# Attention's unit 0 on one core: two of the four key copies are issued by GpSimd instead of SyncE

## The chip, the core and the metric

The kernel runs on one NeuronCore of one Trainium2 chip. A core has five engines that run side by side and meet at semaphores: TensorE (PE, matmuls; PEld is its weight load), VectorE (DVE), ScalarE (ACT), GpSimd (POOL) and SyncE (SP), which here only issues DMAs. The metric is the device time of one execution in microseconds.

## The reference, cut to what matters

The program is two blocks on an `x` of 8 x 512 x 256: an mLSTM-like mixing layer and an MLP, then a cross-attention of 16 heads of 64 and a mixture of 8 experts. The change lies in the cross-attention, which reads a context of the same shape:

```
q = query @ W_Query + B_Query ; k = key @ W_Key + B_Key ; v = value @ W_Value + B_Value
scores = jnp.einsum('bqhd,bkhd->bhqk', q, k) / D ** 0.5
probs = jax.nn.softmax(scores, axis=-1)
out = jnp.einsum('bhqk,bkhd->bqhd', probs, v)
return out.reshape(B, Lq, H * D) @ W_Output + B_Output
```

## The kernel before, in words

Attention (`attention`, L835 to L1290) works through 64 units: 8 batches times 8 pairs of heads. One unit u makes queries, keys and values of two heads (`project`, `project_values` on PE), then 8 score tiles of 128 queries x 512 keys, four per head. Each tile goes PE (`score`, L978), DVE row maximum (L1199), ACT exponential (L1133), DVE reciprocal (L1204), GpSimd scaling (L1174), PE transpose (L991), and a copy to SBUF (L1211 on DVE, L1152 on ACT). Then come values (`weigh_values`) and the output map. The loop is software-pipelined: unit u+1's projections and unit u-1's tail are laid between unit u's score tiles, in an order written out by hand for each engine.

Scores are computed from numbers split in two parts, high and low, so that a matmul over 128 rows holds 64 rows of the one and 64 of the other. The keys come out of PE for both heads at once, 64 partitions each. ACT writes the high part into `k_own[:, 0]` (L1093) and counts `kh`; DVE writes the low part into `k_own[:, 1]` (L1193) and counts `kl`. Then four DMAs (L929, 64 partitions x 4 KB = 256 KB each) copy them into `k2`: head 0, partitions 0 to 63 of `k_own`, to partitions 0 to 63 and to 64 to 127 of `k2`; then head 1, partitions 64 to 127, to both halves likewise. SyncE issues all four, in that order, for each unit, and the first score of a unit waits for all four (L975). `k_own` has one buffer: ACT waits for a unit's copies before it writes the next unit's keys (L1092).

Unit 0 is apart, since nothing is ahead of it to cover its start. PE projects keys, queries and values of unit 0 (L1046 to L1048) and turns the last batch's input (`turn_in`, L1042), then stands at the first score. At that time DVE normalises the last batch (statistics L1251 to L1258, then four instructions at L1263), which needs GpSimd's power (L1167), and makes the low part of the queries (L1186, counts `ql`, for which the first score also waits). GpSimd, after its power, waits for L1263 and adds a bias to the last batch (L1170), then begins the scaling of the tiles (L1174). SyncE, after unit 0's four copies, issues the loads that the attention needs later: the rest of the three projection weights (L907, 768 KB each), the output weights (L909, 1 MB) and the gate weights (L912, 4 bytes at a time).

Of the kernel before, what the change touches and what calls it, by code (L numbers as in the profile page):

```python
# [11 lines left out]
F32 = mybir.dt.float32  # L12
# [4 lines left out]
ALU = mybir.AluOpType  # L17
# [4 lines left out]
P = 128  # L22
B, S, D = 8, 512, 256
N = B * S
TPB = S // P
# [5 lines left out]
AH, AD = 16, 64  # L31
HP = AH // 2
# [13 lines left out]
def sems(ctx, nc, phase, names):  # L46
    return {n: ctx.enter_context(nc.semaphore(f"{phase}_{n}")) for n in names.split()}


def wait_apart(eng, sem, value):  # L50

    eng.wait_ge(sem, value)
    eng.nop(nofuse=True)  # L53
# [313 lines left out]
def wait_count(eng, sem, value):  # L367

    if value > 0:
        eng.wait_ge(sem, value)  # L370
# [462 lines left out]
def attention(nc, c, x_all, xnT_all, ctxT_all, first, after_s, Wq, Wk, Wv, Wo, gate_w, lg, rows, rows_in, out, landed):  # L833
# [3 lines left out]
    with ExitStack() as ctx:  # L837
# [6 lines left out]
        k_own = sb("k_own", [P, 2, S], F32R)  # L844
        k2 = sb("k2", [P, 2, 2, 2, S], F32R)
# [13 lines left out]
        S_BANK, T_BANK, A_BANK, O_BANK, Y_BANK = 0, 2, 4, 6, 7  # L859
        s = sems(ctx, nc, "at", "w scaled q_ps qh ql k_ps kh kl k2 v_ps V s_ps nmax exp rinv pn t_ps "  # L860
                 "pt_v pt_a pv oT y_ps x gT stats mv ve rstd xn tx_ps xT l_ps lg "
                 "in_stats in_mv in_ve in_rstd in_xn in_added in_tx_ps in_xT")
        w_dram = [W.rearrange("(c p) n -> p c n", p=P) for W in (Wq, Wk, Wv)]
        wo_dram = Wo.rearrange("(a p) d -> p a d", p=P)
        ON_ACT = (4, 5)
# [11 lines left out]
        def routed(u, r):  # L877

            return u // HP - 1 if u >= HP and u % HP == r else None

        NORM, APPLY, TURN, GATE, LAST = 1, 2, 3, 4, B - 1
# [20 lines left out]
        with nc.Block() as block:  # L902
            @block.sync
            def _(sp):
                def load_weights():
                    for k in range(3):
                        sp.dma_start(w_rest[:, k, :, :], w_dram[k][:, :, W_EARLY * P:HP * P]).then_inc(s["w"], 16)  # L907
                    sp.wait_ge(first["loaded"], 16 * 6)
                    sp.dma_start(wo_s[:, :, :], wo_dram).then_inc(first["loaded"], 16)  # L909
                    with nc.allow_non_contiguous_dma("8 gate weights per row"):  # L910
                        for k in range(DC):
                            sp.dma_start(gT[:, k, :], gate_w.rearrange("e (k p) -> p k e", p=P)[:, k, :]  # L912
                                         ).then_inc(s["gT"], 16)

                def store_rows(b):
                    sp.wait_ge(s["xn"], b + 1)
                    rv = rows.rearrange("(b k h p) d -> b p k h d", k=2, h=2, p=P)
                    for k in range(2):
                        sp.dma_start(rv[b, :, k, :, 0:D], ctxT_all[:, k, b * S:b * S + S].rearrange(
                            "p (h d) -> p h d", d=D)).then_inc(rows_in, 16)  # L920
                    sp.dma_start(out[0:N, :].rearrange("(b t p) d -> b p t d", p=P, t=TPB)[b],
                                 x_all[:, b * TPB:(b + 1) * TPB, :]).then_inc(landed, 16)

                for u in range(U):
                    sp.wait_ge(s["kh"], u + 1)
                    sp.wait_ge(s["kl"], u + 1)
                    for h in range(2):
                        for half in range(2):
                            sp.dma_start(k2[AD * half:AD * half + AD, u % 2, h, :, :].bitcast(F32),  # L929
                                         k_own[AD * h:AD * h + AD, :, :].bitcast(F32)).then_inc(s["k2"], 16)  # L930
                    if u == 0:
                        load_weights()
                    if routed(u, TURN) is not None:
                        store_rows(routed(u, TURN))
                store_rows(LAST)

            @block.tensor
            def _(pe):
# [32 lines left out]
                def score(u, j):  # L971
                    wait_count(pe, s["exp"], NBL * u + j - 1)
                    if j == 0:
                        pe.wait_ge(s["ql"], u + 1)
                        pe.wait_ge(s["k2"], 64 * (u + 1))  # L975
                    h, q = j // TPB, P * (j % TPB)
                    for part in range(2):
                        ins = pe.matmul(ps[:, S_BANK + j % 2, :], q2[:, u % 2, h, q:q + P], k2[:, u % 2, h, part, :],  # L978
                                        start=part == 0, stop=part == 1)
                    ins.then_inc(s["s_ps"], 1)  # L980
# [69 lines left out]
                for u in range(U + 1):  # L1050
                    for j in range(NBL):
                        if there(u):
                            score(u, j)
                            if j >= 2:
                                turn(u, j - 2)
                        if j < 2 and there(u - 1):
                            turn(u - 1, NBL - 2 + j)
                        if j < 2 and there(u + 1):
                            project(u + 1, j)
                        if j == 2 and there(u - 1):  # L1060
                            weigh_values(u - 1)
                        if j == 4 and there(u + 1):
                            project_values(u + 1)
                        if j in (5, 6) and there(u - 1):
                            output(u - 1, j - 5)
                        if j in (3, 7) and there(u):
                            if j == 3 and there(u + 1) and u % HP in (TURN, GATE):
                                pe.wait_ge(s["kl"], u + 2)
                            if routed(u, TURN) is not None:
                                turn_rows(routed(u, TURN), j // 4)  # L1070
                            if routed(u, GATE) is not None:
                                if routed(u, GATE) == 0 and j == 3:
                                    pe.wait_ge(s["gT"], 16 * DC)
                                map_gates(routed(u, GATE), j // 4)
# [6 lines left out]
            def _(act):  # L1081
# [7 lines left out]

                def keys(u):  # L1090
                    act.wait_ge(s["k_ps"], u + 1)
                    wait_count(act, s["k2"], 64 * u)  # L1092
                    act.activation(k_own[:, 0, :], ps[:, A_BANK + 1, :], ACT.Identity,  # L1093
                                   bias=b_s[:, 1, u % HP:u % HP + 1]).then_inc(s["kh"], 1)

# [24 lines left out]

                act.wait_ge(s["scaled"], 1)
                keys(0)
                queries(0)
                values(0)
# [34 lines left out]
            @block.gpsimd  # L1159
            def _(pool):  # L1160
                def spread(b):
                    wait_apart(pool, s["ve"], b + 1)
                    pool.tensor_tensor(rstd[:, :], ve[:, :], c["minus_half"][:, 0:TPB], ALU.pow
                                       ).then_inc(s["rstd"], 1)

                wait_apart(pool, s["in_ve"], 1)
                pool.tensor_tensor(rstd[:, :], ve[:, :], c["minus_half"][:, 0:TPB], ALU.pow).then_inc(s["in_rstd"], 1)  # L1167
                wait_apart(pool, s["in_xn"], 1)
                x_last = x_all[:, LAST * TPB:(LAST + 1) * TPB, :]
                pool.tensor_tensor(x_last, x_last, after_s[:, :].rearrange("p (a d) -> p a d", a=1).broadcast_to(  # L1170
                    [P, TPB, D]), ALU.add).then_inc(s["in_added"], 1)
                for n in range(NBL * U):
                    wait_apart(pool, s["rinv"], n + 1)
                    pool.tensor_scalar(Pr[:, n % 4, :], Pr[:, n % 4, :], rinv[:, n % 4:n % 4 + 1], 1.0,  # L1174
                                       ALU.mult, ALU.mult).then_inc(s["pn"], 1)
                    if n % NBL == NBL - 1 and routed(n // NBL, NORM) is not None:
                        spread(routed(n // NBL, NORM))
                spread(LAST)

            @block.vector  # L1180
            def _(dve):
# [31 lines left out]

                def add_out(u, half):
                    dve.wait_ge(s["y_ps"], 2 * u + half + 1)
                    if u == LAST * HP:
                        dve.wait_ge(s["in_added"], 1)
                    at = (u // HP) * TPB + 2 * half
                    xv = x_all[:, at:at + 2, :].rearrange("p t d -> p (t d)")
                    dve.tensor_tensor(xv, ps[:, Y_BANK - half, :], xv, ALU.add).then_inc(s["x"], 1)  # L1220
# [583 lines left out]
```

## Time and profile before

| | us |
|---|---|
| median of 3 runs (lowest, highest) | 1828.46 (1826.79, 1832.12) |
| the profiled execution's own time | 1826.98 |
| its span | 1825.2 |
| PE busy | 1657.8 (91%) |
| DVE, ACT, POOL busy | 1209.9, 842.8, 606.4 |
| the key copies (L929), 256 issues, issue to landing | 4.1 |

The span is what the trace covers; the execution takes 1.8 us more. Attention lies from about 427 us to 1597 us in it. Idle time is told with what ended it: `<-DMA at_k<-at_k_own` means that the copy from `k_own` to `k2` was the last thing that the engine waited for. A DMA has two times: that of the instruction which issues it, and that from its issue to its landing, when the semaphore has its full count. PEclk is the clock that the throttle granted to TensorE, 1.00 for 2.4 GHz and 0.50 for 1.2 GHz.

### The profile page before, as it was taken

The page shows a single profiled execution, that of the slowest core. Times are in us where ns is not written, and L with a number is a line of the kernel's source. Part 1 is how long each engine was busy: PE and PEld are TensorE (multiplying, and loading weights), DVE is VectorE, ACT ScalarE, POOL GpSimd, SP SyncE. Part 2 cuts the span into 40 slices and gives each one's busy share as a digit, 9 for nine tenths or more (in the row PEclk, how much of TensorE's full clock was granted, in tenths as well). Part 3 has the DMA queues.
Part 4 walks back from the last instruction along what each step waited for, and adds up shares of the span by engine and source line. Part 5 has one row for each costly group of instructions (what it writes and reads, how often), then busy time and mean ns, then how long its engine had stood idle before and what let it go on. Part 6 is the DMA issues. An engine that isn't in the chain of part 4 may idle for free. (4 is left out here: it accounts for less than half of the span.)

```text
span 1825.2 us, 25796 instructions
## 1 busy us (share of the span) xinstructions
PE 1657.8 (91%) x8789; PEld 1126.1 (62%) x8789; DVE 1209.9 (66%) x2690; ACT 842.8 (46%) x1870; POOL 606.4 (33%) x730
## 2 busy tenths in 40 slices
PE   6569999998999999999999999999999999973583
PEld 4447777756666666666666666666666666642352
DVE  6445655534777777777777786777777777748770
ACT  3324343433555555555555555555555555531110
POOL 2144444431232323322332332232332333220485
PEclk9669999999999999999999999999999999985697
DMA  8100000004222323232322232232323232213244
GB/s 261 31 24 12 12 12 1 1 0 122 51 66 53 87 47 70 47 93 47 70 70 62 54 88 53 52 88 47 70 47 93 47 70 70 57 37 98 46 85 57
DMA packets 68961, 109.46 MB, mean 60 GB/s; under 512 B 18400, under 2 KB 50400, under 8 KB 68832
## 3 DMA queue, kind: packets, MB, share of 16 engines
q1 hardware_dynamic: 62688, 99.29, 22.3%
q0 software_dynamic: 6144, 8.52, 2.9%
q8 instruction: 72, 1.18, 0.3%
q14 instruction: 57, 0.47, 0.1%
HBM read 27.84 MB, written 12.85 MB: 22 GB/s over the span
## 5 line engine op out<-in xcount | busy, mean ns | idle before, releaser
L1174 POOL TENSOR_SCALAR at_Pr<-at_Pr,at_rinv 128x512 f32<-128x512 f32 x512 | 354.2, 692 | 825.2 <-DVE at_rinv L1204 825.2
L1133 ACT ACTIVATE at_Pr<-at_ps,at_nmax 128x512 f32<-128x512 f32 x512 | 352.0, 687 | 529.8 <-DVE at_nmax L1199 528.1
L1199 DVE TENSOR_REDUCE at_nmax<-at_ps 128x1 f32<-128x512 f32 x512 | 351.1, 686 | 149.5 <-PE at_ps L978 137.9
L978 PE MATMUL at_ps<-at_k,at_q 128*128 128x512 f32 x1024 | 420.0, 491 | 6.3 <-DMA at_k<-at_k_own 4.6
L991 PE MATMUL at_ps<-k_ident,at_Pr 128*128 128x128 f32 x2048 | 309.7, 274 | 4.0 <-POOL at_Pr L1174 4.0
L991 PEld LDWEIGHTS at_ps<-k_ident,at_Pr 128*128 128x128 f32 x2048 | 250.7, 140 | 89.3 <-POOL at_Pr L1174 27.1
L1211 DVE COPY at_PT<-at_ps 128x512 f32<-128x512 f32 x384 | 261.4, 681 | 0.0
L978 PEld LDWEIGHTS at_ps<-at_k,at_q 128*128 128x128 f32 x1024 | 174.4, 190 | 126.3 <-issue 116.3
L1003 PE MATMUL at_ps<-at_PT,at_V 128*64 128x512 f32 x1024 | 235.5, 602 | 0.9 <-DVE at_PT L1211 0.9
L1204 DVE RECIPROCAL at_rinv<-at_rsum 128x1 f32<-128x1 f32 x512 | 83.3, 163 | 159.9 <-ACT at_Pr L1133 157.9
L1003 PEld LDWEIGHTS at_ps<-at_PT,at_V 128*64 128x64 f32 x1024 | 68.1, 137 | 122.7 <-issue 121.6
L1013 PE MATMUL at_ps<-at_wo,at_oT 128*128 128x256 f32 x512 | 131.6, 380 | 0.8 <-ACT at_oT L1103 0.8
L465 PE MATMUL mm_ps<-mx_w,mm_hT 128*128 128x256 f32 x512 | 119.6, 382 | 0.0
L455 PE MATMUL mm_ps<-m_xnT,mx_w 128*128 128x512 f32 x256 | 111.2, 592 | 1.3 <-ACT m_xnT L604 1.3
L465 PEld LDWEIGHTS mm_ps<-mx_w,mm_hT 128*128 128x128 f32 x512 | 94.3, 190 | 16.1 <-issue 3.8
L1186 DVE SCALAR_TENSOR_TENSOR at_q<-at_ps,m_b_all,at_q 64x512 fp32r<-64x512 f32 x128 | 96.0, 750 | 5.5 <-ACT at_q L1086 2.8
L1133 ACT ACTIVATION_READ_ACCUMULATOR at_Pr<-at_ps,at_nmax 128x1 f32 x512 | 98.7, 193 | 0.0
L956 PE MATMUL at_ps<-m_ctxT,at_w_rest 128*128 128x512 f32 x192 | 90.9, 595 | 4.0 <-ACT m_xnT L1108 4.0
L966 PE MATMUL at_ps<-at_w_rest,m_ctxT 128*128 128x128 f32 x768 | 93.6, 275 | 0.0
L1013 PEld LDWEIGHTS at_ps<-at_wo,at_oT 128*128 128x128 f32 x512 | 87.4, 190 | 8.3 <-ACT at_oT L1103 1.7
L956 PE MATMUL at_ps<-m_xnT,at_w_rest 128*128 128x512 f32 x192 | 90.3, 593 | 0.0
L966 PEld LDWEIGHTS at_ps<-at_w_rest,m_ctxT 128*128 128x128 f32 x768 | 89.5, 192 | 0.0
(246 smaller groups left out, 2053.7 us busy)
## 6 DMA issues: line engine op xcount, KB each, us to landing
at_k<-at_k_own SPq DMA_DIRECT2D x256, 256.0 KB, 4.1
k_x<-in_x SPq DMA_DIRECT2D x8, 512.0 KB, 8.4
mg_ctx<-in_ctx SPq DMA_DIRECT2D x8, 512.0 KB, 8.8
mx_ctxn<-in_ctx SPq DMA_DIRECT2D x8, 512.0 KB, 3.8
rows<-m_ctxT SPq DMA_DIRECT2D x16, 256.0 KB, 2.6
out<-k_x SPq DMA_DIRECT2D x8, 512.0 KB, 3.5
r_w<-in_L_ffn_w SPq DMA_DIRECT2D x16, 256.0 KB, 5.4
mx_w<-in_L_ffn_w SPq DMA_DIRECT2D x2, 1024.0 KB, 10.0
```

Of the source, the lines that this page charges most:

```text
L455: ins = pe.matmul(ps[:, H_BANK + f % 4, :], w1_s[:, k, P * f:P * f + P], xnT_all[:, k, b * S:b * S + S], start=k == 0, stop=k == DC - 1)
L465: ins = pe.matmul(ps[:, Y_BANK + t // 2, D * (t % 2):D * (t % 2) + D], hT[:, f, P * t:P * t + P], w2_s[:, f, :], start=f == 0, stop=f == F ...
L956: ins = pe.matmul(ps[:, A_BANK + k, :], weights(k, d, hp), src[:, d, b * S:b * S + S], start=d == 0, stop=d == DC - 1)
L966: ins = pe.matmul(ps[:, v_bank(u), P * t:P * t + P], ctxT_all[:, d, b * S + P * t:b * S + P * t + P], weights(2, d, hp), start=d == 0, sto ...
L978: ins = pe.matmul(ps[:, S_BANK + j % 2, :], q2[:, u % 2, h, q:q + P], k2[:, u % 2, h, part, :], start=part == 0, stop=part == 1)
L991: ins = pe.transpose(ps[:, T_BANK + j % 2, P * t:P * t + P], Pr[:, j % 4, P * t:P * t + P], c["ident"][:, :])
L1003: ins = pe.matmul(ps[AD * h:AD * h + AD, O_BANK, :], V[:, u % 2, t, AD * h:AD * h + AD], PT[:, u % 2, h, t, :], start=t == 0, stop=t == TP ...
L1013: ins = pe.matmul(ps[:, Y_BANK - half, D * (t % 2):D * (t % 2) + D], oT[:, P * t:P * t + P], wo_s[:, u % HP, :], start=True, stop=True)
L1133: act.activation(Pr[:, j % 4, :], ps[:, S_BANK + j % 2, :], ACT.Exp, bias=nmax[:, j % 4:j % 4 + 1], accum_out=rsum[:, j % 4:j % 4 + 1]).th ...
L1174: pool.tensor_scalar(Pr[:, n % 4, :], Pr[:, n % 4, :], rinv[:, n % 4:n % 4 + 1], 1.0, ALU.mult, ALU.mult).then_inc(s["pn"], 1)
L1199: dve.tensor_reduce(nmax[:, j % 4:j % 4 + 1], ps[:, S_BANK + j % 2, :], AX.X, ALU.max, negate=True).then_inc(s["nmax"], 1)
L1211: dve.tensor_copy(PT[:, u % 2, j // TPB, :, q:q + P], ps[:, T_BANK + j % 2, :].rearrange("p (t q) -> p t q", t=TPB)).then_inc(s["pt_v"], 1)
```

## The change

Unit 0's copies of head 1 leave SyncE's list. GpSimd issues them, between its power and its addition, after it has waited for `kh` and `kl` of unit 0; they count on a semaphore of their own, `k2_pool`, for which PE's first score waits beside `k2`. Since SyncE now issues two copies of unit 0 and four of each later unit, the counts of `k2` on which PE and ACT wait are 32 lower. The semaphore `in_added` (GpSimd's addition done, awaited by DVE's first output addition of the last batch) is taken away, with its wait. The names: `k2` is `at_k` in the rows of the profile, `k_own` is `at_k_own`.

```diff
@@ sync
-                    for h in range(2):
+                    for h in range(2 if u else 1):
                         for half in range(2):
                             sp.dma_start(k2[AD * half:AD * half + AD, u % 2, h, :, :].bitcast(F32),
@@ tensor, score(u, j)
-                        pe.wait_ge(s["k2"], 64 * (u + 1))
+                        pe.wait_ge(s["k2"], 64 * (u + 1) - 32)
+                        if u == 0:
+                            pe.wait_ge(s["k2_pool"], 32)
@@ scalar, keys(u)
-                    wait_count(act, s["k2"], 64 * u)
+                    wait_count(act, s["k2"], 64 * u - 32)
@@ gpsimd
                 pool.tensor_tensor(rstd[:, :], ve[:, :], c["minus_half"][:, 0:TPB], ALU.pow).then_inc(s["in_rstd"], 1)
+                pool.wait_ge(s["kh"], 1)
+                wait_apart(pool, s["kl"], 1)
+                for half in range(2):
+                    pool.dma_start(k2[AD * half:AD * half + AD, 0, 1, :, :].bitcast(F32),
+                                   k_own[AD:2 * AD, :, :].bitcast(F32)).then_inc(s["k2_pool"], 16)
                 wait_apart(pool, s["in_xn"], 1)
...
-                    [P, TPB, D]), ALU.add).then_inc(s["in_added"], 1)
+                    [P, TPB, D]), ALU.add)
@@ vector, add_out(u, half)
-                    if u == LAST * HP:
-                        dve.wait_ge(s["in_added"], 1)
```

GpSimd's order at the head of attention, before: `at_rstd` is the power of the last batch's variance, `k_x` its rows of x, `at_Pr` the tiles of probabilities.

```order
112 L1167 TENSOR_TENSOR at_rstd<-at_ve,k_minus_half 128x4 [waits at_in_ve]
113 L1170 TENSOR_TENSOR k_x<-k_x,m_after 128x1024 [waits at_in_xn]
114 L1174 TENSOR_SCALAR at_Pr<-at_Pr,at_rinv 128x512 [waits at_rinv] x80
115 L1163 TENSOR_TENSOR at_rstd<-at_ve,k_minus_half 128x4 [waits at_ve]
116 L1174 TENSOR_SCALAR at_Pr<-at_Pr,at_rinv 128x512 [waits at_rinv] x64
```

And now:

```order
112 L1169 TENSOR_TENSOR at_rstd<-at_ve,k_minus_half 128x4 [waits at_in_ve]
113 L1173 DMA at_k<-at_k_own 64x1024 [waits at_kh,at_kl]
114 L1173 DMA at_k<-at_k_own 64x1024
115 L1177 TENSOR_TENSOR k_x<-k_x,m_after 128x1024 [waits at_in_xn]
116 L1181 TENSOR_SCALAR at_Pr<-at_Pr,at_rinv 128x512 [waits at_rinv] x80
```

The two DMAs stand behind the power and ahead of the addition and of the first scaling.

SyncE's order at the same place, before:

```order
40 L929 DMA at_k<-at_k_own 64x1024 [waits at_kl,at_kh]
41 L929 DMA at_k<-at_k_own 64x1024 x3
42 L907 DMA at_w_rest<-in_L_xattn_W_Query 128x2x768
43 L907 DMA at_w_rest<-in_L_xattn_W_Key 128x2x768
44 L907 DMA at_w_rest<-in_L_xattn_W_Value 128x2x768
45 L909 DMA at_wo<-in_L_xattn_W_Output 128x8x256 [waits m_loaded]
46 L912 DMA at_gT<-in_L_ffn_gate_w 128x8x1 x2
47 L929 DMA at_k<-at_k_own 64x1024 [waits at_kl,at_kh]
```

And now:

```order
40 L929 DMA at_k<-at_k_own 64x1024 [waits at_kl,at_kh]
41 L929 DMA at_k<-at_k_own 64x1024
42 L907 DMA at_w_rest<-in_L_xattn_W_Query 128x2x768
43 L907 DMA at_w_rest<-in_L_xattn_W_Key 128x2x768
44 L907 DMA at_w_rest<-in_L_xattn_W_Value 128x2x768
45 L909 DMA at_wo<-in_L_xattn_W_Output 128x8x256 [waits m_loaded]
46 L912 DMA at_gT<-in_L_ffn_gate_w 128x8x1 x2
47 L929 DMA at_k<-at_k_own 64x1024 [waits at_kl,at_kh]
```

The weight loads stand two copies nearer to the front; the next unit's copies (row 47) are unchanged.

## Rows read from the trace of the kernel before

**Rows 1.** The page, busy time and share of the span of each engine.

```profile
PE 1657.8 (91%) x8789; PEld 1126.1 (62%) x8789; DVE 1209.9 (66%) x2690; ACT 842.8 (46%) x1870; POOL 606.4 (33%) x730
```

**Rows 2.** Busy time by stretch; last columns PEclk, DMA share, GB/s. Attention.

```profile
core 0: us, PE busy (x) PEld busy (x) DVE busy (x) ACT busy (x) POOL busy (x), PEclk, DMA share, GB/s
427.00:1597.00 1170.00, 1159.53 (x6185) 771.83 (x6186) 862.33 (x1797) 642.91 (x1465) 355.82 (x509) 1.00 0.29 67
```

**Rows 3.** Waits of PE, 427 to 470 us: total, times, longest.

```profile
PE at_ps L978 <- DMA at_k<-at_k_own: 4.6, 2, 4.1
```

**Rows 4.** PE's timeline: start, us, instruction, idle before it.

```profile
428.88 1.88 PE L956 MATMUL at_ps<-m_xnT,m_w_first 128*128 128x512 f32 x4
...
437.73 0.70 PE L978 MATMUL at_ps<-at_k,at_q 128*128 128x512 f32 x2 [4.14 <-DMA at_k<-at_k_own]
438.27 3.29 PE L956 MATMUL at_ps<-m_xnT,m_w_first 128*128 128x512 f32 x4
440.58 1.71 PE L978 MATMUL at_ps<-at_k,at_q 128*128 128x512 f32 x2
```

**Rows 5.** Timeline of DVE, POOL and SP around unit 0's keys.

```profile
429.94 0.75 DVE L1193 SCALAR_TENSOR_TENSOR at_k_own<-at_ps,m_b_all,at_k_own 128x512 fp32r<-128x512 f32 x1
431.06 1.38 DVE L1263 TENSOR_SCALAR m_xnT<-k_x,at_mv,at_rstd 128x256 f32<-128x256 f32 x4 [0.37 <-POOL at_rstd L1167]
432.48 1.51 DVE L1186 SCALAR_TENSOR_TENSOR at_q<-at_ps,m_b_all,at_q 64x512 fp32r<-64x512 f32 x2
...
430.01 1.02 POOL L1167 TENSOR_TENSOR at_rstd<-at_ve,k_minus_half 128x4 f32<-128x4 f32 x1 [24.32 <-DVE at_ve L1258]
432.59 2.35 POOL L1170 TENSOR_TENSOR k_x<-k_x,m_after 128x1024 f32<-128x1024 f32 x1 [1.57 <-DVE m_xnT L1263]
440.36 0.69 POOL L1174 TENSOR_SCALAR at_Pr<-at_Pr,at_rinv 128x512 f32<-128x512 f32 x1 [5.42 <-DVE at_rinv L1204]
...
433.98 1.19 SPq L907 DMA_DIRECT2D at_w_rest<-in_L_xattn_W_Query  x1
```

**Rows 6.** The copies' line, unit 0: issue durations in ns, and to landing.

```profile
L929 SPq DMA_DIRECT2D at_k<-at_k_own x4: 528/620/1265, 430.8 to 432.7; - x4
...
DMA to landing us min/median/max: 3.0/4.2/4.9
```

**Rows 7.** By stretch, while unit 0's copies move; columns as in rows 2.

```profile
432.00:434.60 2.60, 1.59 (x13) 1.21 (x12) 1.94 (x4) 1.73 (x4) 2.01 (x1) 1.00 0.99 191
434.60:435.50 0.90, 0.00 (x0) 0.00 (x0) 0.00 (x0) 0.88 (x2) 0.34 (x1) 1.00 1.04 296
435.50:436.70 1.20, 0.00 (x0) 0.00 (x0) 0.00 (x0) 0.50 (x1) 0.00 (x0) 1.00 0.98 227
```

**Rows 8.** GpSimd's indirect gathers among the experts; the second one's idle time before it.

```profile
1705.95 0.96 POOL L1554 DMA_INDIRECT ex_xg<-rows,ex_idx_get  x1 [0.30 <-issue]
...
L1554 POOL DMA_INDIRECT ex_xg<-rows,ex_idx_get x32: 942/946/1234, 1704.4 to 1788.4; - x32
...
DMA to landing us min/median/max: 2.7/2.8/3.8
```

**Rows 9.** By stretch, behind unit 0's first score; columns as in rows 2.

```profile
433.60:437.70 4.10, 0.00 (x0) 0.00 (x0) 0.39 (x1) 2.36 (x3) 1.34 (x1) 1.00 1.05 221
437.70:438.50 0.80, 0.77 (x3) 0.67 (x4) 0.03 (x1) 0.00 (x0) 0.00 (x0) 1.00 0.82 284
438.50:439.50 1.00, 1.00 (x2) 0.33 (x1) 0.66 (x1) 0.30 (x1) 0.00 (x0) 0.54 0.63 224
439.50:442.00 2.50, 2.50 (x5) 1.21 (x4) 0.16 (x1) 0.87 (x3) 0.69 (x1) 0.50 0.96 377
442.00:445.00 3.00, 3.00 (x13) 1.80 (x12) 2.56 (x5) 2.43 (x5) 0.07 (x1) 1.00 1.03 390
```

**Rows 10.** Unit 1's copies and its first score, from the timeline.

```profile
446.82 3.83 SPq L929 DMA_DIRECT2D at_k<-at_k_own  x4
...
454.35 0.30 PEld L978 LDWEIGHTS at_ps<-at_k,at_q 128*128 128x128 f32 x2 [0.65 <-ACT at_Pr L1133]
454.38 0.70 PE L978 MATMUL at_ps<-at_k,at_q 128*128 128x512 f32 x2 [0.44 <-DMA at_k<-at_k_own]
```

More of the change, by code:

```diff
@@ L861, in attention @@
                  "pt_v pt_a pv oT y_ps x gT stats mv ve rstd xn tx_ps xT l_ps lg "
-                 "in_stats in_mv in_ve in_rstd in_xn in_added in_tx_ps in_xT")
+                 "in_stats in_mv in_ve in_rstd in_xn k2_pool in_tx_ps in_xT")
         w_dram = [W.rearrange("(c p) n -> p c n", p=P) for W in (Wq, Wk, Wv)]
```

## The prediction

> **What bounds the kernel now.** I read the page's busy times first: PE is busy for 91% of the span [rows 1]. Then busy time by stretch: over the 1170 us of attention PE is busy for 1159.5 us at the full clock, so that it has 10.5 us of idle time in all 64 units together [rows 2]. A change to one unit's copies can only touch part of that. The waits of PE for 427 to 470 us say which part: the first score of a unit stood behind the key copies twice, 4.6 us in all, 4.1 of them once [rows 3]. The timeline places the 4.1 us ahead of unit 0's first score, which starts at 437.73 after 4.14 us of idle time, and so puts PE's last work before at 433.59 [rows 4]. The small one, 0.44 us, is unit 1's [rows 10]. There is a second loss behind the first. The granted clock is 1.00 while PE idles and for 0.8 us after, then 0.50 to 442 us [rows 9]: PE had stood for 4.1 us and worked for 0.9 before it fell to the 1.2 GHz level. The same four matmuls of L956 take 1.88 us at the full level and 3.29 at the half one, and a score's two 1.71 against 0.70 [rows 4], 2.4 us together.
>
> **What holds the first score.** Four conditions meet there. PE is ready at 433.59. The low part of the queries (L1186) ends at 432.48 + 1.51 = 433.99 [rows 5]. The keys' low part (L1193) ends at 430.69, and SyncE issues from 430.8. The copies land between 430.8 + 3.0 = 433.8 and 432.7 + 4.9 = 437.6 [rows 6]. So the last copy holds it, and no change to the copies alone can start it before about 434.0: the most that the wait can give is 437.7 - 434.0 = 3.7 us.
>
> **Why the last copy is late.** Issuing is not what takes longest. Its four issues are through at 432.7 + 1.3 = 434.0, and the last copy lands 3.6 us later. While the copies move, the DMA engines are busy at 0.98 to 1.04 of their time [rows 7]; 1 MB at some 213 GB/s takes 4.9 us, and from 432.0 that is 436.9, 0.7 before the last landing. Whether GpSimd or SyncE issues the third and fourth, the same 1 MB goes through the same 16 engines. Yet a full share of engine time isn't a full rate: the same share carries 390 GB/s when weights arrive [rows 9], and among the copies there is a stretch at 296 GB/s between 191 and 227 [rows 7]. By its place (second 256 KB out, third coming in) that is where the second copy, from the lower partitions to the upper, overlaps with the third, from the upper to the lower. So two copies with nothing in common go faster side by side than two which share a half. Two queues could widen that overlap.
>
> **The steps.**
> - Taken from SyncE: two issues, 0.66 and 1.26 us. No wait ends on them as issues. But the loads behind them (L907) begin at about 432.1 instead of 433.98 [rows 5], and the first 768 KB then compete with GpSimd's copies instead of following them.
> - Added to GpSimd: two plain DMAs. The trace has none; bounds from both sides. The nearest row is the indirect gather, 0.95 us and 0.30 to the next, landing after 2.8 [rows 8]; a gather of 128 rows of 264 floats is 135 KB, 0.6 us at 213 GB/s, which leaves 2.2 us that aren't transfer. SyncE's first copy leaves 3.0 - 1.2 = 1.8 [rows 6]. So a GpSimd copy costs between 0.5 us (as SyncE's issue) and 1.25 us of GpSimd, and starts to move between 0 and 0.4 us later than one of SyncE would. I take the gather's, as the same engine issues it.
> - GpSimd is free at 430.01 + 1.02 = 431.03 [rows 5], the keys are there by then, so issue 1 is at 431.1 and issue 2 at 432.35. Alone they would land at 431.1 + 2.2 + 1.2 = 434.5 and at 435.75. They are not alone.
> - If the engines' time is what is short (a packet from one queue, then one from the other), GpSimd's copies start to move at 431.1 + 2.2 - 0.7 = 432.6, when SyncE's have 1.5 of 2 copies left. 1.5 beside 1.5 at 1.2 us a copy take 3.6 us, to 436.2; the last half copy beside as much of the weights 1.1, to 437.3, landing at 438.0. That is 0.4 us later than now.
> - If the halves are what is short, the second and third copy run together at up to 296 instead of 213 GB/s: 512 KB in 1.8 instead of 2.5 us; the fourth shares with the weights, which the 390 GB/s rows let pass beside it. Landing at about 436.8, 0.8 us earlier.
> - I take a point nearer the second, since rows 7 show its overlap: 437.2, 0.4 us earlier.
> - The addition (L1170) is pushed from 432.59 to behind issue 2, about 433.7, and ends at about 436.0. The first scaling (L1174) is at 440.36 [rows 5]. 4.3 us of cover; were GpSimd's two DMAs to hold it for more than that, each us over would delay the first tile by one.
> - PE's and ACT's lowered counts and the removed `in_added` wait are bookkeeping; `in_added` was raised more than 1000 us before its use. One more wait at the first score costs at most some 0.1 us. Together nothing.
>
> **What is late next.** A gain must pass unit 1, whose copies are issued at 446.82 by SyncE and end on a PE wait of 0.44 us [rows 10]. All of unit 0's chain moves with its first score, the keys of unit 1 too, but their copies queue behind the weights in SyncE's queue. These leave earlier now as well, so I let the gain through; the 0.44 us is at once what a later start can hide. From unit 2 on PE has no copy waits, so what arrives there stays. The sum: -0.4 us on the profiled execution's own time, 1826.98 - 0.4 = 1826.6. That execution is 1.5 us under the median of the runs shown, which gives 1828.1.
>
> The Trainium skill (DMA: Bandwidth & Descriptors, "Issuing engines are not separate DMA queues") says that spreading DMAs over engines saves only the issuing sequencer's time, as all run on the same 16 DMA engines. By it alone the landing stays at 437.6 or gets worse by what the weights take. The 0.98 to 1.04 shares agree with it; the 296 GB/s in between says that the order in which copies meet matters too.
>
> **Rivals.**
> 1. *Copies overlap well and the clock dip goes.* The first score starts at 436.7 or before, PE idles 3.1 us, and the half-level stretch doesn't come: -1.0 - 2.4 = -3.4 us, 1825.1. For it: the dip followed on one idle stretch of 4.1 us. Against: the dip also came with PE back at work for 0.9 us, so a slightly shorter idle time may not do. Chance 0.2.
> 2. *GpSimd's copies start late (slower).* Place: between 431.1 and 432.44, where DVE runs four SBUF to SBUF instructions (L1263). If GpSimd can't write its DMAs while they run, issue 1 is at 432.44, 1.3 us later, and the last landing at 438.0 + 1.3 = 439.3. That decides once GpSimd's second copy starts to move later than about 434.5. Price: 1.6 us, less the 0.44 of unit 1's slack, plus between 0 and 2.4 for a half-level stretch that gets longer: +1.2 to +3.6, 1831 at the middle. For it: the trace has no DMA issue of GpSimd beside such work of DVE, so nothing excludes it. Against: GpSimd's power runs at 430.01 beside DVE's L1193 without either being held [rows 5]. Chance 0.2. The Trainium skill (SBUF — State Buffer, "SBUF: two separate sides") calls something like it a trap: a DVE instruction in a two-port mode keeps GpSimd from writing its DMA descriptors. No row here shows the two side by side.
> 3. *It doesn't do what it says:* the copies interleave so that the landing is where it was, ±0.2 us: inside the forecast.
>
> **Numbers.** Forecast (first score within 1 us of 437.73, time within 1.5 us of 1828.1) 0.6, rival 1 0.2, rival 2 0.2. A measurement of this kernel tells about 0.3%, 5.5 us, from no change; the three runs shown spread over 5.3. No case here reaches 5.5 us: the full wait and dip are 3.7 + 2.4 = 6.1 us. So same 0.88, faster 0.07, slower 0.05, mostly the measurement's own. The range takes rival 1's 1825.1 and rival 2's upper end of 1832.
>
> **What the profile after would show.** GpSimd's two DMAs at about 431.1 and 432.4, the weights' first issue at about 432.1, the first score between 436.7 and 438.2, and unit 1's wait for its copies under 1 us. A rate above 250 GB/s between 433 and 435.5 speaks for the halves, one of about 213 for the engines. Wrong would be: a GpSimd DMA that takes over 2 us, a first score after 439 or before 436, or a change of over 3 us from unit 2 on, where nothing was touched.

## The result, and the profile after

The changed kernel takes 1834.94 us (median of 22 runs, 1830.13 to 1836.39) against 1828.65 of the kernel before: a ratio of 1.0027, 95% interval 1.0021 to 1.0033. That is slower by some 5 us (4.9 by the ratio; the two medians are 6.3 apart), above the forecast's range, where no change was forecast. Two runs that stand far outside all others, one of the kernel before at 8227.63 us and one of experiment 1 at 2907.54 us, count in the medians and not in the ratios.

Waits of PE from 427 to 480 us (total, times, longest), where [rows 3] had 4.6, 2, 4.1:

```profile
PE at_ps L980 <- DMA at_k<-at_k_own: 8.9, 1, 8.9
```

The timeline of the changed kernel around unit 0's keys, to be read beside [rows 4, 5]. Each row is start, us, instruction, idle time before it:

```profile
434.77 1.09 PE L1044 MATMUL at_ps<-k_ident,m_xnT 128*128 128x128 f32 x8
444.76 1.19 PE L980 MATMUL at_ps<-at_k,at_q 128*128 128x512 f32 x2 [8.90 <-DMA at_k<-at_k_own]
445.75 3.62 PE L956 MATMUL at_ps<-m_xnT,m_w_first 128*128 128x512 f32 x4
...
433.60 1.46 POOL L1173 DMA_DIRECT2D at_k<-at_k_own  x2 [0.31 <-issue]
435.06 2.38 POOL L1177 TENSOR_TENSOR k_x<-k_x,m_after 128x1024 f32<-128x1024 f32 x1
...
432.20 0.75 DVE L1200 SCALAR_TENSOR_TENSOR at_k_own<-at_ps,m_b_all,at_k_own 128x512 fp32r<-128x512 f32 x1
...
433.05 1.16 SPq L929 DMA_DIRECT2D at_k<-at_k_own  x2
434.25 0.65 SPq L907 DMA_DIRECT2D at_w_rest<-in_L_xattn_W_Query  x1
```

The whole of attention lies 2.26 us later in this execution than in the one before, which comes from earlier stages, where nothing was changed. So from here on times of unit 0 are counted from the end of the keys' low part: 430.69 before, 432.95 here, "the keys" for short. The first score was at 437.73 - 430.69 = 7.0 us from the keys and is now at 444.76 - 432.95 = 11.8. GpSimd's issues are early and cheap. The landings aren't, as its line shows:

```profile
L1173 POOL DMA_DIRECT2D at_k<-at_k_own x2: 556/728/899, 433.6 to 434.5; - x2
...
DMA to landing us min/median/max: 5.9/8.0/10.1
```

The first lands at 433.6 + 5.9 = 439.5, the second at 434.5 + 10.1 = 444.6, 11.7 from the keys; SyncE's copies took 3.0 to 4.9 [rows 6]. What moved in between, by DMA queue (q1 is SyncE's, q0 is GpSimd's; packets, MB, share of the 16 engines), from 434.2 to 437.2:

```profile
q1 hardware_dynamic: 145, 0.52, 105.1%
```

from 437.25 to 438:

```profile
q0 software_dynamic: 44, 0.18, 84.0%
q1 hardware_dynamic: 15, 0.00, 1.1%
```

from 438.75 to 440.2:

```profile
q1 hardware_dynamic: 151, 0.46, 99.5%
q0 software_dynamic: 5, 0.00, 0.2%
```

and from 440.5 to 444:

```profile
q1 hardware_dynamic: 220, 0.63, 73.5%
q0 software_dynamic: 79, 0.26, 29.4%
```

These four windows show the loss. Up to 440.5 the queues take turns: SyncE's two copies, GpSimd's first, then most of W_Query's 768 KB. GpSimd's second copy (0.26 MB) moves only from about 440.5, beside the end of W_Query and W_Key; its issue was over by 435.06. (q0's 5 packets of the third window are the small ones that count the first copy's semaphore.)

Busy time by stretch (PE, PEld, DVE, ACT, POOL, then PEclk, DMA share, GB/s):

```profile
435.90:440.60 4.70, 0.00 (x0) 0.00 (x0) 0.36 (x1) 2.36 (x3) 1.54 (x1) 1.00 0.98 241
440.70:444.70 4.00, 0.00 (x0) 0.00 (x0) 0.00 (x0) 0.00 (x0) 0.00 (x0) 0.50 1.03 272
444.70:450.80 6.10, 6.04 (x9) 3.17 (x10) 1.40 (x3) 2.14 (x4) 0.69 (x1) 0.50 1.05 307
450.90:460.00 9.10, 8.33 (x50) 5.96 (x48) 7.72 (x16) 4.38 (x10) 2.77 (x4) 1.00 0.46 99
```

The granted clock falls after 4.7 us without a matmul and is at the half level from 440.6 to 450.9 instead of for 3.4 us. Part of that passes while PE stands; what falls on work costs 1.0 us more than before: GpSimd's scaling of tile 4 is 5.8 us later from the keys than before, the first score 4.8. From tile 4 to the last batch this distance stays: it is 5.8 at unit 8 and 5.4 at unit 56. So 4.8 + 1.0 = 5.8 us of this pair of executions come from unit 0's start, beside the ratio's 4.9 (3.8 to 6.0).

In attention's last unit the clock falls once more, for 3.4 us, which it did not at that place before. The first row is the changed kernel's, the second that of the kernel before:

```profile
1614.90:1618.20 3.30, 3.23 (x10) 1.49 (x12) 1.85 (x5) 1.34 (x4) 1.40 (x3) 0.50 0.00 0
1612.60:1616.00 3.40, 2.83 (x17) 1.94 (x16) 2.90 (x7) 2.14 (x5) 1.00 (x2) 1.00 0.00 0
```

The distance is 7.0 us at the last tile and 6.2 at the end of the program. The same fall is in experiments 1, 3, 5, 6 and 10, where GpSimd issues copies with its addition right behind them, and in none of the others. Why stays open.

### The profile page after: what moved, and what is told of

Same layout as the page of the kernel before. It is cut to its first block and busy times, and to the rows that moved or that the text cites. A ratio compares the mean times of both kernels' runs of the same rounds, so it can differ in the third digit from the quotient of the medians.

```text
span 1833.7 us, 25796 instructions
## 1 busy us (share of the span) xinstructions
PE 1661.6 (91%) x8789; PEld 1129.0 (62%) x8789; DVE 1210.2 (66%) x2690; ACT 843.6 (46%) x1870; POOL 607.3 (33%) x732
## 5 line engine op out<-in xcount | busy, mean ns | idle before, releaser
L465 PEld LDWEIGHTS mm_ps<-mx_w,mm_hT 128*128 128x128 f32 x512 | 94.3, 190 | 16.1 <-issue 3.8
L956 PE MATMUL at_ps<-m_ctxT,at_w_rest 128*128 128x512 f32 x192 | 90.8, 595 | 4.0 <-ACT m_xnT L1110 4.0
L956 PE MATMUL at_ps<-m_xnT,at_w_rest 128*128 128x512 f32 x192 | 90.3, 593 | 0.0
## 6 DMA issues: line engine op xcount, KB each, us to landing
mx_w<-in_L_ffn_w SPq DMA_DIRECT2D x2, 1024.0 KB, 10.1
```

What stands on the lines that cost most here:

```text
L465: ins = pe.matmul(ps[:, Y_BANK + t // 2, D * (t % 2):D * (t % 2) + D], hT[:, f, P * t:P * t + P], w2_s[:, f, :], start=f == 0, stop=f == F ...
L956: ins = pe.matmul(ps[:, A_BANK + k, :], weights(k, d, hp), src[:, d, b * S:b * S + S], start=d == 0, stop=d == DC - 1)
```

## The experiments

Each kernel changes the changed kernel; "changed" below stands for it. Experiments 2, 3, 5, 6, 8 and 10 are one execution each: they are read by where things lie in the trace, not by their times.

**1. The weight loads held back.** SyncE issues them when GpSimd's copies have landed.

```diff
                     if u == 0:
+                        sp.wait_ge(s["k2_pool"], 32)
                         load_weights()
```

> SyncE waits for GpSimd's two copies before it issues the weight loads, so nothing follows its two copies in its queue. Times are from the end of the keys' low part (L1200 of the changed kernel), where the changed kernel has GpSimd's copies landing 6.6 and 11.7 us later and the first score at 11.8 (before: 7.0). Turns (the DMA engines empty what stands in one queue before they turn to the other, so GpSimd's second copy waited for W_Query): the first copy still lands at 6.5, the second right behind it at 7.7 to 8.5, first score 8, total about 3 us less than the changed kernel's. Held by DVE, by the addition, or slow in itself: the second copy still starts 2 us behind the end of the first, lands at 10 to 11, first score 10.5 to 11, total within 1.5 us of the changed kernel's.

Ratio to the kernel before 1.0002 (0.9988 to 1.0016), with 1831.38 us as the median of its 10 runs. GpSimd's copies, issued just as early (0.6 and 1.5 us from the keys), landed 5.9 and 7.0 from the keys:

```profile
L1174 POOL DMA_DIRECT2D at_k<-at_k_own x2: 558/731/904, 432.0 to 432.9; - x2
...
DMA to landing us min/median/max: 5.3/5.4/5.4
```

The first score was at 7.1: its whole loss is gone with nothing changed on GpSimd. Both copies were even earlier than the theory of turns had them (6.5, and 7.7 to 8.5). For all that it isn't the kernel before: the loads now end later, unit 1's copies land behind them at 24.8 us from the keys instead of 23.6, and by unit 8 GpSimd's scaling is 2.7 us later from the keys than before, where changed is 5.8 later.

**2. The addition moved away.** GpSimd's L1177 goes behind unit 0's eighth scaling.

```diff
-                wait_apart(pool, s["in_xn"], 1)
-                ... pool.tensor_tensor(x_last, x_last, after_s ..., ALU.add)
                 for n in range(NBL * U):
...
+                    if n == NBL - 1:
+                        wait_apart(pool, s["in_xn"], 1)
+                        ... pool.tensor_tensor(x_last, x_last, after_s ..., ALU.add)
```

> GpSimd's addition to the last batch moves from right behind the two DMAs to behind unit 0's eighth scaling. Addition to blame (it keeps GpSimd from finishing its DMAs' work behind the issue): first packets of copy 1 about 2 us earlier, first score at 8 to 9.5 us from the end of the keys' low part instead of 11.8. Turns, DVE, or slow in itself: 11.8 within 0.5.

First score at 11.4, one execution of 1835.29 us. The theory of the addition wanted 8 to 9.5, so the addition isn't the cause.

**3. Issue behind DVE's normalisation.**

```diff
-                wait_apart(pool, s["kl"], 1)
+                pool.wait_ge(s["kl"], 1)
+                wait_apart(pool, s["in_xn"], 1)
```

> GpSimd issues its copies only when DVE's four instructions of the last batch's normalisation are done, 1.1 us later than in the changed kernel. Held by DVE: nothing gets later, as the DMA could not start before that anyway: first score 11.8 us within 0.3. Turns: the first copy lands as before, since it waits for SyncE's second copy, which is through at 4 us; the second waits for the weights as before: 11.8 within 0.5 too. Slow in itself (a fixed 3.7 us from issue to first packet): all 1.1 us later, 12.9.

First score at 12.7; 1836.57 us. The issues start 2.5 us from the keys, 1.9 later than in changed (my 1.1 was too low):

```profile
435.77 1.33 POOL L1174 DMA_DIRECT2D at_k<-at_k_own  x2 [2.16 <-DVE m_xnT L1269]
```

DVE's four instructions were over, and still the first packets came 4.3 us behind the issue, against 3.7 in changed. So a hold by these four falls as the cause; experiment 5 shows the same from the other side. The number is also beyond what turns gave, and nearer that of "slow in itself". It fits turns only with a step that I had not thought of: SyncE's copies were through 3.8 us from the keys, before GpSimd's work was ready (about 2.5 + 1.5, by experiment 5), so W_Query took the turn and both of GpSimd's copies stood behind it. Their first packets came at 6.8, W_Query's at 3.9.

**4. ScalarE issues instead of GpSimd.**

```diff
                 keys(0)
+                act.wait_ge(s["kl"], 1)
+                for half in range(2):
+                    act.dma_start(k2[AD * half:AD * half + AD, 0, 1, :, :].bitcast(F32),
+                                  k_own[AD:2 * AD, :, :].bitcast(F32)).then_inc(s["k2_pool"], 16)
                 queries(0)
...
```

GpSimd's two DMAs and its waits for them are gone.

> ScalarE issues head 1's two copies in GpSimd's place, between the high part of the keys and the queries, after the wait for kl. Turns between any two queues: the second copy still waits for the weights, first score 10 to 12 us from the end of the keys' low part. Something of GpSimd's own path (its software queue): ScalarE's copies start as early as SyncE's and share the engines with them, first score 6.5 to 7.5, total within 2 us of the kernel before.

Ratio 0.9996 (0.9984 to 1.0009); the last copy lands at 6.9, first score at 6.9. The keys are at 431.79 here. From 433 to 438 us both queues move about as much (q10 is ScalarE's; SyncE's 0.61 MB are its two copies and the start of W_Query):

```profile
q1 hardware_dynamic: 188, 0.61, 58.8%
q10 hardware_dynamic: 160, 0.52, 46.4%
```

Such a long window can't tell sharing from turns. The short ones inside it can. From 433 to 434.3:

```profile
q10 hardware_dynamic: 64, 0.26, 104.4%
```

and from 434.4 to 435:

```profile
q1 hardware_dynamic: 44, 0.18, 95.7%
q10 hardware_dynamic: 12, 0.00, 4.9%
```

First all of ScalarE's first copy (64 packets, 0.26 MB) goes and nothing of SyncE's, then SyncE's first. Packet by packet the four copies run from 1.2 to 2.4 (ScalarE), 2.6 to 3.9 (SyncE), 3.2 to 4.5 (ScalarE) and 4.3 to 5.6 us (SyncE), W_Query from 5.5. So these two queues take turns of about one copy as well, with edges that overlap. The theory of turns had expected the second copy behind the weights here; it wasn't, since ScalarE's copies had their turns before W_Query was at the head of SyncE's queue. What GpSimd's queue had and this one hadn't is a first turn that came late: its first packets stood behind both of SyncE's copies. ScalarE also issued 0.6 us earlier (0.03 against 0.65) and its first packets were 1.2 us behind the issue; no run has it issue at GpSimd's time. The second issuer gains nothing: the same 1 MB ends when it did.

The first score is 0.1 us nearer to the keys than before, but GpSimd's scaling is 0.6 us farther from tile 2 on: the half-level clock lasted 6.8 us here (436.8 to 443.6), against 3.4 before, with PE idle for 4.0 us against 4.1.

**5. GpSimd's queue alone.** It issues all four copies, the loads wait for them; the counts on which PE and ScalarE wait follow.

```diff
-                for half in range(2):
-                    pool.dma_start(k2[AD * half:AD * half + AD, 0, 1, :, :].bitcast(F32), ...
+                for h in range(2):
+                    for half in range(2):
+                        pool.dma_start(k2[AD * half:AD * half + AD, 0, h, :, :].bitcast(F32), ...
```

> GpSimd issues all four copies of unit 0, SyncE none, and the weight loads wait until they have landed: GpSimd's path with nothing beside it. Times from the end of the keys' low part. Turns: with no other queue in the way GpSimd's first packets start 1.5 to 2 us behind its first issue, at 2.2 to 2.7, the four follow each other at 1.2 us, last landing 7.5 to 8.5. Slow in itself: first packets 3.4 to 3.7 us behind the issue as in the changed kernel, at 4.1 or later, last landing 9.5 or later.

```profile
L1176 POOL DMA_DIRECT2D at_k<-at_k_own x4: 527/545/897, 432.1 to 434.0; - x4
...
DMA to landing us min/median/max: 3.4/4.1/4.8
```

First packets at 2.1 us from the keys, 1.5 behind the first issue; the last landing at 434.0 + 4.8 = 438.8, 7.3 from the keys (431.44; all figures rounded), first score at 7.5. Alone, GpSimd's path is 0.4 us behind SyncE's, not 5. It isn't slow in itself. DVE's four instructions ran from 0.4 to 1.8 us from the keys, beside the issues as in changed, and the first packets came all the same at 2.1, not at 4.3: rival 2's hold can't be the 3.7 us between issue and first packet there.

**6. W_Query in two DMAs.** The same bytes in the same order.

```diff
-                    for k in range(3):
+                    for d in range(DC):
+                        sp.dma_start(w_rest[:, 0, d, :], w_dram[0][:, d, W_EARLY * P:HP * P]).then_inc(s["w"], 16)
+                    for k in (1, 2):
```

> The changed kernel with SyncE's first load, 768 KB of W_Query, issued as two DMAs of 384 KB; the same bytes in the same order. Turn of one DMA at a time: GpSimd's second copy gets in behind the first half, its first packets 1.2 to 1.6 us earlier than the 7.5 us of the changed kernel, first score at 10.0 to 10.7 instead of 11.8. Backlog (whatever SyncE's queue holds when GpSimd's work arrives goes first, however it is cut): 11.8 within 0.5.

First score at 9.0 instead of 11.8, 1832.02 us. The second copy's first packets moved from 7.5 to 6.5, its landing from 11.7 to 8.9:

```profile
L1175 POOL DMA_DIRECT2D at_k<-at_k_own x2: 556/728/899, 433.4 to 434.3; - x2
...
DMA to landing us min/median/max: 5.8/6.6/7.3
```

With a backlog of bytes it would have stayed where it was. How SyncE's work is cut into DMAs decides, as turns of about one DMA have it; the gain was larger than expected, since the second copy also moved faster once begun.

**7. Control: SyncE issues all four,** the other edits stay.

```diff
-                    for h in range(2 if u else 1):
-                        for half in range(2):
+                    for h, half in ((0, 0), (0, 1), (1, 0), (1, 1)):
...
+                                     ).then_inc(s["k2_pool" if u == 0 and h else "k2"], 16)
...
```

GpSimd's two DMAs and its waits for them are gone.

> Control: all the changed kernel's edits except who issues: SyncE issues all four copies again, head 1's on the semaphore k2_pool, PE waits for both, the added GpSimd waits are gone and in_added stays away. Every theory of the copies: as the kernel before, first score 7.0 us from the end of the keys' low part, ratio 1.000 within 0.001. If the semaphore bookkeeping or the missing in_added wait were the cause: slower by up to 5 us.

Ratio 0.9997 (0.9988 to 1.0007), first score at 7.1. The counts and the missing `in_added` are nothing; what is left is who issues, and with it when each copy has its turn.

**8. The order of the copies,** on top of the control: lower to lower, upper to upper, lower to upper, upper to lower.

```diff
-                    for h, half in ((0, 0), (0, 1), (1, 0), (1, 1)):
+                    for h, half in ((0, 0), (1, 1), (0, 1), (1, 0)):
```

> All four copies issued by SyncE, in the order lower to lower, upper to upper, lower to upper, upper to lower, in every unit. If copies which share no half overlap faster (two such pairs stand side by side now instead of one): the last landing 0.4 to 0.9 us earlier than the 6.9 us of before. If the engines' time is all that counts: 6.9 within 0.2.

Last landing 6.97, first score 7.1; 1828.31 us. The theory that the halves set the rate falls as far as the last landing goes: that of the four copies stayed where it was. The fast stretch of [rows 7] is no overlap either. From 434.6 to 435.5 in the kernel before:

```profile
q1 hardware_dynamic: 86, 0.27, 104.1%
```

That is the size of one copy: the third's packets run from 3.9 to 4.8 us from the keys, when the second's have been through since 3.8. In the new order it is the second copy (upper to upper, 2.6 to 3.5 us) that takes 0.9 us, and the others 1.1 to 1.3; the last packet goes at 5.9 us instead of 6.1, and the last copy lands no earlier. Why one of the four is faster is open.

**9. The wait split,** on top of the control. Unit 0's first score needs head 0 only; unit 1's keys wait for head 1's copies, as in experiment 10.

```diff
-                        if u == 0:
-                            pe.wait_ge(s["k2_pool"], 32)
...
+                    if u == 0 and j == TPB:
+                        pe.wait_ge(s["k2_pool"], 32)
```

> As the control, but unit 0's first score waits for head 0's two copies only, and head 1's two are awaited at the fifth tile. Unit 0 starts at 4.7 us instead of 7.0. Theory that what is gained at unit 0 stays: 2.3 us faster, up to 4.5 with the half-clock stretch gone, ratio 0.9975 to 0.999. Rival: unit 1's copies can't start before the weights in SyncE's queue are through, 17.3 us from the keys' low part, so that unit 1's first score waits 2.3 us longer (2.7 instead of 0.4) and the ratio is 1.000 within 0.001.

Ratio 1.0014 (1.0005 to 1.0023): slower. The first score is 2.3 us nearer to the keys, and unit 1 gives it back:

```profile
440.06 0.70 PE L980 MATMUL at_ps<-at_k,at_q 128*128 128x512 f32 x2 [1.85 <-DMA at_k<-at_k_own]
440.60 3.09 PE L956 MATMUL at_ps<-m_xnT,m_w_first 128*128 128x512 f32 x4
...
458.97 1.19 PE L980 MATMUL at_ps<-at_k,at_q 128*128 128x512 f32 x2 [2.79 <-DMA at_k<-at_k_own]
459.96 1.05 PE L993 MATMUL at_ps<-k_ident,at_Pr 128*128 128x128 f32 x4
460.81 3.62 PE L956 MATMUL at_ps<-m_xnT,at_w_rest 128*128 128x512 f32 x4
```

Unit 1's copies stood behind the loads in SyncE's queue: issued from 14.5 us from the keys instead of 16.1, they landed by 23.5 as before (23.6). So PE's second wait grew from 0.44 to 2.79 us, and the half-level clock came at both places: L956's four matmuls take 3.62 us at unit 1, 1.88 before. By unit 8 GpSimd's scaling is 2.7 us later from the keys than before. The rival had the mechanism, but not this price: it said 1.000.

**10. The same split with GpSimd issuing head 1,** and ScalarE guarded by a wait.

```diff
@@ scalar, keys(u)
                     wait_count(act, s["k2"], 64 * u - 32)
+                    if u == 1:
+                        act.wait_ge(s["k2_pool"], 32)
```

> The changed kernel (GpSimd issues head 1's copies), but the first score waits for head 0's two and the fifth tile for head 1's; ScalarE waits for head 1's before it writes unit 1's keys. First score at 5.3 us instead of 11.8, GpSimd's copies still land at 6.6 and 11.7, ScalarE's wait costs at most 0.5 us. Late landing is the whole loss: the fifth tile never waits, and unit 1's copies are what is late next (PE waits 2 to 4 us there), total 1829 to 1832. If the loss had another part (GpSimd's time, its addition): tiles 2 to 8 of unit 0 come later than 1.9 us ahead of the kernel before.

1831.03 us. First score at 5.3; the copies landed at 6.5 and 11.5, as late as in changed, and PE waited for copies only at the first scores of units 0 and 1:

```profile
PE at_ps L980 <- DMA at_k<-at_k_own: 6.3, 2, 3.9
```

ScalarE's wait was 1.7 us, more than expected. Tiles 2 to 8 of unit 0 came 3.0 to 3.2 us ahead of the kernel before. With the first score's wait for them gone, the late landings cost unit 0 nothing. Of the 3.0 us, 1.7 are the earlier first score; the rest comes with the clock, which stayed at the full level in unit 0 though PE had stood for 2.4 us:

```profile
437.30:444.00 6.70, 6.18 (x22) 3.52 (x23) 4.29 (x8) 3.33 (x8) 1.39 (x2) 1.00 1.02 287
```

PE's wait of 3.9 us at unit 1 takes it back: by unit 8 the scaling is 2.3 us later from the keys than before.

**11. Split, and the last two loads behind unit 1's copies,** on top of experiment 9.

```diff
                     if u == 0:
                         load_weights()
+                    if u == 1:
+                        load_rest()
```

`load_rest` holds the loads of the output and gate weights, which leave `load_weights`.

> SyncE issues all four copies, unit 0's first score waits for head 0's two only, and the loads of the output and gate weights move behind unit 1's copies, so that nothing stands before these in SyncE's queue. Theory (unit 1's copies were held by the loads ahead of them, as the first split showed with 2.79 us): first score at 4.7 us from the end of the keys' low part, unit 1's copies issued at 14 us start within 1.2, their last lands by 21, PE waits for them under 0.5 us, ratio 0.997 to 0.999. If it is SyncE's issue or the copies themselves: unit 1 waits 2 us or more again and the ratio is 1.000 or above.

1823.83 us (1823.62 to 1826.73), ratio 0.9977 (0.9968 to 0.9986): faster than both kernels. SyncE's timeline and PE's waits from 427 to 480 us:

```profile
447.12 3.12 SPq L930 DMA_DIRECT2D at_k<-at_k_own  x4
450.29 1.16 SPq L911 DMA_DIRECT2D at_wo<-in_L_xattn_W_Output  x1
451.49 2.98 SPq L914 DMA_DIRECT2D at_gT<-in_L_ffn_gate_w  x2
```

```profile
PE at_ps L984 <- DMA at_k<-at_k_own: 1.9, 1, 1.9
```

Unit 1's copies, issued at 14.1 us from the keys, landed by 20.9. PE waits for copies once and 1.9 us in all, against twice and 4.6 [rows 3]. The trace shows less of the gain than the ratio, which stands for 4.2 us (2.6 to 5.9): GpSimd's scaling is 2.0 us nearer to the keys than before from tile 2 of unit 0, 1.9 at unit 8, and the end of the program 2.6. The profiled execution (1826.73 us) was the slowest of the 11.

## Why the prediction was wrong, by its steps

- **What bounds and what holds the first score:** right. The first score was the one place that counted, and the last copy what held it.
- **GpSimd's issue:** right in kind, dearer than measured. Said 1.25 us each, measured 0.90 and 0.56. That a GpSimd copy starts to move 1.5 us behind its issue (432.6 against 431.1) is what experiment 5 has with the queue alone.
- **The step that failed:** the one that let GpSimd's copies share the engines as soon as they were ready, "a packet from one queue, then one from the other", with the last landing at 438.0, or 7.3 from the keys. It put the first packets at 1.9 from the keys; they came at 4.3, behind both of SyncE's copies, and the second copy's at 7.5, behind most of W_Query. The sum lacked these two waits for a turn, for a last landing at 11.7. Experiments 1, 5 and 6 show it: without the loads 7.0, alone 7.3, with the load cut in two 8.9. The weight loads, 2.0 us earlier, had been named as rivals for the engines, but priced at half a copy's time; they set the turn: before, W_Query stood behind all the copies.
- **The halves:** the other half of the same step. The point that I took between the two prices leaned on the 296 GB/s of [rows 7], read as an overlap of the second and third copy. It was the third copy alone (experiment 8). The new order gives the last landing nothing, and a second issuer in experiment 4 nothing either.
- **The rule of the Trainium skill** (DMA: Bandwidth & Descriptors, "Issuing engines are not separate DMA queues"), that issuing from several engines saves only the sequencer's time, agrees with experiment 4 to 0.1 us in the last landing. But GpSimd's last copy landed 4.8 us later than SyncE's had: here a second issuer cost time. The rule was worth more than the 0.4 us that I set against it.
- **Rival 2 (slower)** had the sign and not the cause. Its price was +1.2 to +3.6 us by a hold of DVE; experiment 3 takes the hold away and the delay stays, and in experiment 5 DVE's work is there and the delay isn't. That a first score after 439 (8.3 from the keys) would refute the forecast was said, and it came at 11.8.
- **The clock:** the dip was named as a second loss. It lasted 10.3 us instead of 3.4 and cost 1.0 us more on work; I had allowed 0 to 2.4. That it grew by the longer idle time alone isn't shown: it lasted 6.8 us in experiments 4, 5 and 8 with PE idle for 4.0 to 4.6 us, and 3.4 in experiments 1 and 7 with 4.2.
- **The cover of the addition:** right. It ended at 437.44, 10.4 us before the first scaling.
- **What is late next:** named, and wrongly let through. I took unit 1's 0.44 us as small and its copies as moving along. Experiment 9 shows that they don't: 2.3 us gained at unit 0 became a loss of 0.14% until experiment 11 moved the loads. In the changed kernel this didn't decide: its unit 1 came so late that PE waited for no copy there, as the forecast's "under 1 us" had it.
- **The measurement:** 0.3% was held to be out of reach of any case, because I bounded the gain side by the wait there was (6.1 us, which is itself over the 5.5) and the loss side by rival 2 alone. A wait can grow by what stands in another queue, and the loads (768 KB each, 7.3 to 8.4 us to landing) were in the trace.

What stays open: why GpSimd's first copy missed the turn behind SyncE's first. With the queue alone its packets come at 2.1 us from the keys, and SyncE's second copy began only at 2.6 and went first. ScalarE's second copy did get in between SyncE's two. Whether this is GpSimd's queue or the later issue is not tested. Experiment 6 says that the turn ends with a DMA and not with a number of bytes, from one cut and one execution; experiment 3 needs that reading after the fact. Also open is why the queues move at once, and a copy slower, beside W_Key (3.1 us against 1.3).

## What to carry to other kernels

Before a DMA is moved to another engine to save its issue time, look whether issue or transfer ends last; here the engines were busy at 1.0 of their time, so there was nothing to save. Then ask what the old queue will send in its place: a bulk load that used to stand behind the urgent copies can come to stand in front. To start sooner, wait for less (only the copies that the first tile reads) and put bulk loads behind the next urgent ones too, together, since the one without the other lost here.

## What was not expected of the hardware

- Two DMA queues moved in turns of about one DMA: ScalarE's and SyncE's copies followed each other one by one (experiment 4), and GpSimd's second copy stood 6.0 us from issue to first packet, behind most of a load of 768 KB.
- GpSimd's plain DMA of 256 KB is cheap to issue: 0.78 to 0.90 us for the first and 0.53 to 0.56 for those behind it, against 0.95 for one of its indirect gathers and 0.30 of idle time before the next [rows 8].
- PE's idle time before the first score does not tell by itself whether the clock falls, or for how long. After 1.9 us (experiments 9 and 11) and 4.1 us (the kernel before) the half level lasted 3.4 us, after 2.4 us (experiment 10) it didn't come, with 4.0 us (experiment 4) it lasted 6.8 and with 8.9 us (changed) 10.3.
